# One stage of a graph network on Trainium2: harmonics of the plane products read from PSUM, fewer VectorE products, radial products scaled in place

## The reference, cut to what matters

```
out_s = [w_ss * s * y0,  w_vv0 * (dot(v, y1) / sqrt(3))]
out_v = [(w_sv * s) * y1,  w_vs * v * y0,  w_vv1 * (cross(v, y1) / sqrt(2))]
```

## Time and profile before

| what | us |
|---|---|
| median of three runs (6443.19 to 6455.58) | 6447.02 |
| the profiled execution | 6445.45 |
| its span | 6443.7 |
| DVE busy in the span (75%) | 4808.7 |
| PE busy (75%) | 4855.9 |
| POOL busy (66%) | 4230.3 |
| ACT busy (36%) | 2316.4 |

### The profile page before, as it was taken

One profiled execution on the slowest core, in us unless ns is written; L12 is line 12 of the kernel. 1 busy time (PEld: TensorE's weight loads), 2 busy tenths in 40 slices (PEclk: granted clock), 3 DMA queues, 4 the chain that ended last, 5 costly groups with the idle time before them and its releaser, 6 DMA issues. The chain is left out here.

```text
span 6443.7 us, 162517 instructions
## 1 busy us (share of the span) xinstructions
PE 4855.9 (75%) x45499; PEld 3778.9 (59%) x45500; DVE 4808.7 (75%) x11056; ACT 2316.4 (36%) x6999; POOL 4230.3 (66%) x4250
## 2 busy tenths in 40 slices
PE   6666667488888888888888769877766677777775
PEld 3444445377777777777777757644444464444445
DVE  5777776489989899898998764477777756666665
ACT  1100002266666666666666567400100021000001
POOL 5777775177767777777777347277777727777772
PEclk8888888699999999999999979888888887777777
DMA  3333332133333333333333247222222212222221
GB/s 108 92 92 92 92 92 69 44 94 90 92 89 92 92 89 92 90 91 92 89 92 90 66 148 229 61 73 72 72 72 72 72 38 69 69 69 69 69 69 38
DMA packets 401459, 545.15 MB, mean 85 GB/s; under 512 B 144998, under 2 KB 283382, under 8 KB 401244
## 3 DMA queue, kind: packets, MB, share of 16 engines
q0 software_dynamic: 193920, 331.22, 20.7%
q1 hardware_dynamic: 207452, 212.84, 11.3%
HBM read 464.79 MB, written 78.90 MB: 84 GB/s over the span
## 5 line engine op out<-in xcount | busy, mean ns | idle before, releaser
L816 POOL DMA_INDIRECT e_rows<-tab,e_idx x2424 | 2291.8, 945 | 814.1 <-issue 682.3
L1085 POOL DMA_INDIRECT acc<-tabx,a_idx x1616 | 1682.1, 1041 | 870.4 <-issue 465.2
L861 PE MATMUL e_wps<-e_w,e_hidT 64*128 64x192 f32 (+1 forms) x4848 | 792.9, 461 | 877.1 <-DVE e_hidT L932 874.5
L861 PEld LDWEIGHTS e_wps<-e_w,e_hidT 64*128 64x128 f32 x4848 | 539.7, 250 | 1081.1 <-DVE e_hidT L932 967.8
L846 PE MATMUL e_win<-e_feat,e_ohy 128*32 128x96 f32 (+1 forms) x19392 | 1026.5, 330 | 23.4 <-DVE e_feat L926 21.9
L846 PEld LDWEIGHTS e_win<-e_feat,e_ohy 128*32 128x32 f32 x19392 | 706.6, 131 | 454.2 <-issue 296.5
L917 DVE TENSOR_TENSOR e_feat<-e_wps,e_rows 128x256 f32<-128x256 f32 x606 | 257.3, 425 | 836.7 <-DMA e_rows<-tab,e_idx 758.7
L926 DVE TENSOR_TENSOR e_feat<-e_wps,e_rows 128x384 f32<-128x384 f32 (+1 forms) x1616 | 719.2, 496 | 0.0
L1148 PE MATMUL a_c<-acc,a_buffer 128*128 128x64 f32 (+1 forms) x4848 | 624.7, 272 | 121.8 <-ACT a_buffer L1126 121.8
L835 ACT ACTIVATE e_idx<-src 128x4 int32 (+1 forms) x606 | 123.3, 204 | 1603.1 <-DMA e_rows<-tab,e_idx 1580.1
L1148 PEld LDWEIGHTS a_c<-acc,a_buffer 128*128 128x128 f32 (+1 forms) x4848 | 590.3, 192 | 143.9 <-issue 143.9
(11 more groups left out here) (252 smaller groups left out, 7851.1 us busy)
## 6 DMA issues: line engine op xcount, KB each, us to landing
h_d<-a_buffer SPq DMA_DIRECT2D x202, 322.0 KB, 2.5
s_hin<-h_d SPq DMA_DIRECT2D x202, 322.0 KB
e_rows<-tab,e_idx POOLq DMA_INDIRECT x2424
e_ein<-in_e64T SPq DMA_DIRECT2D x202, 128.0 KB
acc<-tabx,a_idx POOLq DMA_INDIRECT x1616
a_ein<-in_e_h SPq DMA_DIRECT2D x202, 64.0 KB
e_ein<-in_e16T SPq DMA_DIRECT2D x202, 32.0 KB
tab<-p_rows SPq DMA_DIRECT2D x36, 160.0 KB
```

Source lines behind the costliest of these rows:

```text
L816: pool.indirect_dma_start(out=rows[:, s, t, :], out_offset=None, in_=k.tab0, in_offset=bass.IndirectOffsetOnAxis(ap=idx[:, s, t:t + 1], ax ...
L861: mm = pe.matmul(wps[:, e, 2 * u + j, 0:WC], hidT[half, edges], w2[half, :], start=True, stop=True)
L1085: pool.indirect_dma_start(out=rows[:, b, q, :], out_offset=None, in_=table, in_offset=bass.IndirectOffsetOnAxis(ap=idx[:, b, end, q:q + 1] ...
```

## The change: what it does

- The nine harmonics are laid out with one of them negated, so that one subtraction of planes gives two terms of the dot product or components of the cross product together: `y13_t` has 13 columns, of which 0 to 8 are the planes, 9 to 11 the plain harmonics, 12 is y0. ScalarE negates column 4 in SBUF once for each group, and waits for that write.
- `head` has eight operations: the add; one joint product for both scalar products (512 elements); the plane product with harmonics from `wps[224:233]`; the product for the w_vs part; one subtraction of 512 elements; the cross product's weights; an add of 128 elements; the dot product's weights.
- ScalarE scales the radial products in place in `wps` and copies the nine harmonics behind them. `wy` is gone.
- `mid` still has nine: the plane product reads its harmonics from `c2[192:201]`, and waits for `yc_ready`, which ScalarE signals after the copy that stands behind the scalars of the value row. The reduction and the two subtractions become two subtractions of 256 elements and an add of 128, which waits for the first of them.
- Two halves in `z` change places, and so do the rows of two weight matrices.

```diff
-    HEAD, MID, TAIL = 10, 9, 2
+    HEAD, MID, TAIL = 8, 9, 2
-        ybuf = scratch(U, TPG, 10)
+        ybuf = scratch(U, TPG, 13)
-        wy = scratch(TPG, 96)
-        vy, red, cr = scratch(TPG, 3, 3, V), scratch(TPG, V), scratch(TPG, 3, V)
+        vy, dc = scratch(TPG, 3, 3, V), scratch(TPG, 4, V)
...
                         act.activation(hrow[:, o, :, 0:S], c2[:, :, 0:S], ACT.Copy).then_inc(hs_ready, 1)
+                    if inside(g, n):
+                        if isinstance(g, int) and g == 1:
+                            hold(act, k, c2_ready, 1)
+                        act.activation(c2[:, :, 192:201], ybuf[:, s, :, 0:9], ACT.Copy).then_inc(yc_ready, 1)
                     take_feat((2,))
...
                         hold(act, k, y_in[b], uses(s, i, 2) * 16 + 16)
+                        act.activation(ybuf[:, b, :, 4], ybuf[:, b, :, 4], ACT.Copy, scale=-1.0).then_inc(minus_ready, 1)
+                        hold(act, k, minus_ready, g + 3)
                         hold(act, k, w_ready, g + 3)
                         for q in range(TPG):
-                            ins = act.activation(wy[:, q, :], wps[:, q, 0:96], ACT.Copy, scale=ybuf[:, b, q, 9:10])
+                            act.activation(wps[:, q, 0:96], wps[:, q, 0:96], ACT.Copy, scale=ybuf[:, b, q, 12:13])
+                        ins = act.activation(wps[:, :, 224:233], ybuf[:, b, :, 0:9], ACT.Copy)
                         ins.then_inc(wy_ready, 1)
...
                     hold(v, k, head_ops, at + 1)
-                    v.tensor_tensor(feat[:, :, 0:S], wy[:, :, 0:S], m[:, :, 0:S], ALU.mult).then_inc(head_ops, 1)
-                    with_planes(vy, mv, y).then_inc(head_ops, 1)
-                    v.tensor_tensor(feat[:, :, 96:160], wps[:, :, 96:160], m[:, :, 0:S], ALU.mult).then_inc(head_ops, 1)
+                    v.tensor_tensor(feat[:, :, 0:192].rearrange("p t (o c) -> p t o c", o=2)[:, :, :, 0:S],
+                                    wps[:, :, 0:192].rearrange("p t (o c) -> p t o c", o=2)[:, :, :, 0:S],
+                                    over(m[:, :, 0:S], 2, 2), ALU.mult).then_inc(head_ops, 1)
+                    with_planes(vy, mv, wps[:, :, 224:233]).then_inc(head_ops, 1)
+                    v.tensor_tensor(pair[:, :, :, 0:V], over(wps[:, :, S:96], 2, 3), mv, ALU.mult).then_inc(head_ops, 1)
                     hold(v, k, head_ops, at + 3)
-                    v.tensor_reduce(red[:, :, :], vy[:, :, 0, :, :].rearrange("p t x c -> p t c x"), AX.X, ALU.add).then_inc(head_ops, 1)
-                    v.tensor_tensor(pair[:, :, :, 0:V], over(wy[:, :, S:96], 2, 3), mv, ALU.mult).then_inc(head_ops, 1)
-                    cross(cr, vy, head_ops)
+                    of = turned_planes(vy)
+                    v.tensor_tensor(dc[:, :, :, :], of[:, :, 0:4, :], of[:, :, 4:8, :], ALU.subtract).then_inc(head_ops, 1)
                     hold(v, k, head_ops, at + 5)
-                    v.tensor_tensor(feat[:, :, S:96], wps[:, :, 160:192], red[:, :, :], ALU.mult).then_inc(head_ops, 1)
-                    hold(v, k, head_ops, at + 8)
-                    v.tensor_tensor(pair[:, :, :, V:2 * V], over(wps[:, :, 192:224], 2, 3), cr[:, :, :, :], ALU.mult).then_inc(head_ops, 1)
+                    v.tensor_tensor(pair[:, :, :, V:2 * V], over(wps[:, :, 192:224], 2, 3), dc[:, :, 1:4, :], ALU.mult).then_inc(head_ops, 1)
+                    v.tensor_tensor(dc[:, :, 0, :], dc[:, :, 0, :], of[:, :, 8, :], ALU.add).then_inc(head_ops, 1)
+                    hold(v, k, head_ops, at + 7)
+                    v.tensor_tensor(feat[:, :, S:96], wps[:, :, 160:192], dc[:, :, 0, :], ALU.mult).then_inc(head_ops, 1)
...
                     hold(v, k, mid_ops, at + 4)
-                    with_planes(ty, vec, y).then_inc(mid_ops, 1)
+                    hold(v, k, yc_ready, g + 1)
+                    with_planes(ty, vec, c2[:, :, 192:201]).then_inc(mid_ops, 1)
                     hold(v, k, mid_ops, at + 6)
                     if not isinstance(g, int) or g >= 2:
                         hold(v, k, z_turned, g * 3 - 3)
-                    v.tensor_reduce(zz[:, :, S:96], ty[:, :, 0, :, :].rearrange("p t x c -> p t c x"), AX.X, ALU.add).then_inc(mid_ops, 1)
-                    cross(pair[:, :, :, V:2 * V], ty, mid_ops)
+                    of = turned_planes(ty)
+                    v.tensor_tensor(zz[:, :, 2 * V:8 * V].rearrange("p t (u w) -> p t u w", u=2)[:, :, :, 0:V], of[:, :, 0:2, :],
+                                    of[:, :, 4:6, :], ALU.subtract).then_inc(mid_ops, 1)
+                    v.tensor_tensor(zz[:, :, 7 * V:11 * V].rearrange("p t (u w) -> p t u w", u=2)[:, :, :, 0:V], of[:, :, 2:4, :],
+                                    of[:, :, 6:8, :], ALU.subtract).then_inc(mid_ops, 1)
+                    hold(v, k, mid_ops, at + 7)
+                    v.tensor_tensor(zz[:, :, S:96], zz[:, :, S:96], of[:, :, 8, :], ALU.add).then_inc(mid_ops, 1)
...
-        "y10_t": edge(i["edge_attr_4"]).reshape(G, TPG, P, 4)[..., [1, 2, 3, 2, 3, 1, 3, 1, 2, 0]]...
+        "y13_t": edge(i["edge_attr_4"]).reshape(G, TPG, P, 4)[..., [1, 3, 1, 2, 2, 2, 3, 1, 3, 1, 2, 3, 0]]...
```

More of the change, by code:

```diff
@@ L1026, in attention_logits @@
         dst_in = [sem(f"a_dst_in{s}") for s in range(U)]
-        w_ready, wy_ready = sem("a_w_ready"), sem("a_wy_ready")
+        w_ready, wy_ready, yc_ready = sem("a_w_ready"), sem("a_wy_ready"), sem("a_yc_ready")
+        minus_ready = sem("a_minus_ready")
         head_ops, mid_ops, tail_ops = sem("a_head_ops"), sem("a_mid_ops"), sem("a_tail_ops")
@@ L1112, in step @@
                         for q in range(TPG):
[L1113 to L1114 removed]
+                            ins = act.activation(z[:, s % 2, q, 160:352].rearrange("p (x w) -> p x w", x=3)[:, :, V:2 * V], vec[:, q, :, :],
+                                                 ACT.Copy, scale=ybuf[:, s, q, 12:13])
                         ins.then_inc(vy_ready, 1)
@@ L1237, in with_planes, with turned_planes @@
                     return v.tensor_tensor(to[:, :, :, :, :].rearrange("p t j x c -> p t j (x c)"), over(of, 2, 3),
-                                           y[:, :, 0:9].unsqueeze(3).to_broadcast([P, TPG, 9, V]).rearrange("p t (j x) c -> p t j x c", j=3),
+                                           y.unsqueeze(3).to_broadcast([P, TPG, 9, V]).rearrange("p t (j x) c -> p t j x c", j=3),
                                            ALU.mult)
-                def cross(to, of, signal):
-                    v.tensor_tensor(to[:, :, 1:3, :], of[:, :, 1, ::-2, :], of[:, :, 2, 0:2, :], ALU.subtract).then_inc(signal, 1)
-                    v.tensor_tensor(to[:, :, 0:1, :], of[:, :, 1, 1:2, :], of[:, :, 2, 2:3, :], ALU.subtract).then_inc(signal, 1)
+                def turned_planes(of):
+                    return of.rearrange("p t j x c -> p t (j x) c")
                 def head(g, s, i):
@@ L1277, in mid @@
                     hold(v, k, sig_ready, g + 1)
-                    v.tensor_tensor(t[:, :, :, :], over(fv[:, :, 0:V], 2, 3), planes(y, 0), ALU.mult).then_inc(mid_ops, 1)
+                    v.tensor_tensor(t[:, :, :, :], over(fv[:, :, 0:V], 2, 3), planes(y, 9), ALU.mult).then_inc(mid_ops, 1)
                     v.tensor_tensor(lk[:, s % 2, :, :, 0:16], rect[:, s % 2, :, :].rearrange("p t (q c) -> p t q c", q=H),
@@ L1303, in tail @@
                     v.wait_ge(hs_ready, g + 1)
-                    v.tensor_tensor(t5[:, :, :, :], over(c2[:, :, S:96], 2, 3), planes(ybuf[:, s % U, :, :], 0), ALU.mult).then_inc(tail_ops, 1)
+                    v.tensor_tensor(t5[:, :, :, :], over(c2[:, :, S:96], 2, 3), planes(ybuf[:, s % U, :, :], 9), ALU.mult).then_inc(tail_ops, 1)
                     if not isinstance(g, int) or g >= 2:
@@ L1881, in _arrays @@
         "e64T": edge(i["edge_attr_64"]).T, "e16T": edge(i["edge_attr_16"]).T, "e8T": edge(i["edge_attr_8"]).T,
-        "y10_t": edge(i["edge_attr_4"]).reshape(G, TPG, P, 4)[..., [1, 2, 3, 2, 3, 1, 3, 1, 2, 0]].transpose(0, 2, 1, 3).reshape(G, P, TPG * 10),
+        "y13_t": edge(i["edge_attr_4"]).reshape(G, TPG, P, 4)[..., [1, 3, 1, 2, 2, 2, 3, 1, 3, 1, 2, 3, 0]].transpose(0, 2, 1, 3).reshape(G, P, TPG * 13),
         "ends_t": np.stack([edge(src).reshape(G, TPG, P), edge(dst, fill=N).reshape(G, TPG, P)], 1).transpose(0, 3, 1, 2).reshape(G, P, 2 * TPG),
@@ L1961, in _arrays @@
     a["L1_c3_c"] = const((96, 64), [(0, 0, (64, 64), 1), (64, 0, (32, 64), r3)])
+    riap = lambda r, c, m: [(r, c, m[2]), (r + V, c, m[1])]
     for name, m in (("L1_c4", three), ("L1_c4_f", factors), ("L1_c4_c", bent(three))):
-        a[name] = _place((P, 64), [(0, 0, m[0])] + pair(64, 32, m))
+        a[name] = _place((P, 64), [(0, 0, m[0])] + riap(64, 32, m))
     for name, m in (("L1_c5", three), ("L1_c5_f", factors), ("L1_c5_c", bent(three))):
-        a[name] = _place((P, 64), pair(0, 0, m) + pair(64, 32, m))
+        a[name] = _place((P, 64), riap(0, 0, m) + riap(64, 32, m))
     w = np.zeros((P, SLOTS, D), f)
```

7 lines of the change are left out of this document (3 added, 4 removed).

## The result

The changed kernel takes 6854.82 us (median of four runs, 6842.4 to 6864.17), the kernel before 6446.41: ratio 1.063, 95% interval 1.0609 to 1.065. That is 408 us more, inside the stated range and near its upper end; 258 were forecast. The profiled execution has a span of 6850.9.

What follows compares the result with a forecast made beforehand. VectorE's closed chain was taken as the bound, with ScalarE and TensorE's just as long. 3.63 + 9.46 = 13.09 us a round, 246 us more over 202 rounds, gave 6693; plus 12, 6705 us; range 6600 to 6890.

Steps and rivals of the forecast that it cites:

- (a): In `mid`, the second plane product waits for ScalarE's harmonics copy: 3.63 us from the head's end against 2.47, VectorE idle 1.16.
- the trip: From the head's end through TensorE and ScalarE, twice each, to VectorE's second plane product in `mid`: 3.63 us a round.
- (b): VectorE from the second plane product to the next head's end: 9.46 us, with 0.40 for two newly exposed own-write waits.
- VectorE as a closed chain: In the kernel before, VectorE waits almost only for its own writes, with gaps of 0.15 to 0.45 us; round 11.87 us.
- the chain over ScalarE and TensorE: Transposes and copies handing one PSUM tile back and forth, through the second map; just as long as VectorE's chain, 11.87 us.
- (c): ScalarE's additions ahead of the `z` copies: negation, its wait and harmonics copy into `wps`, some 0.47 us, hidden.
- the sign that was named for being wrong in (c): TensorE's waits for ScalarE, not for VectorE, coming ahead of the transposes of `feat`.
- The tie and the clock: Over the whole kernel, 12 us (0.06 a round) added because the chains tie and the clock may fall at times.
- Rival 2: TensorE's clock falls as its busy share drops to 0.77; low half the time, 6800 to 6940, taken as 6850; chance 0.12.
- the case that was held the likeliest: The new wait in `mid` lengthens VectorE's round to 13.09 us; 6705 us, own range 6670 to 6890, chance 0.75.
- The skill's rules: For VectorE, PSUM sources costing more would give about 6757; semaphores costing nothing, about 6624; the prediction followed neither.

Runs made afterwards that it cites:

- the repeated-matmul kernel: Changed kernel with the first map's three products of tile 0 done twice in each round; 6636.85 us, ratio 1.0302 to the kernel before.
- the chain edits alone: Kernel before with only TensorE's waits reordered and the scaling of the gated vectors split; ratio 1.0014 on a slower chip, repeats 1.0031 and 1.002.
- the 109: Gain over the kernel before with SBUF harmonics, negation moved, TensorE waits reordered, vector scaling split and head reordered, on the changed kernel: 6331.48 against 6440.51 us.
- the wait alone: Kernel before with only the harmonics copy into c2 and the second plane product reading it there, so waiting for it; 6980.48 us, ratio 1.0845.

## Why the prediction was right in kind and short in size

- **The new wait in `mid` (a), right.** It is there in nearly every round, behind ScalarE's copy, and taking it away from this place gives back 337 of 408 us. At full clock the trip is 3.72 us (head's end 2504.98 to 2508.70), 3.63 were summed; VectorE's idle time 1.23, 1.16 were summed.
- **VectorE from there to the next head's end (b), too long.** 9.11 us on average, 9.46 summed. The two exposed own waits are 0.15 us each (one is 2516.23 + 0.68 to 2517.05), not 0.20; and the gap between add and first product is 0.15 (2512.92 + 0.82 to 2513.89), not 0.45. At full clock the round is 12.85 us by the repeated-matmul kernel, 13.09 were summed.
- **VectorE as a closed chain, wrong.** The gap of 0.45 us ahead of the head's first product was read as a wait for VectorE's own add. That product also waits for ScalarE's radial scaling, and two further waits stand behind that one. In the kernel before it starts 0.53 us after the scaling has ended, at the median and within 0.01 us in most rounds, while the gap behind the add varies from 0.29 to 0.45 us in eight rounds of ten. Here the scaling ends at 2511.74 + 1.02 = 2512.76:

```profile
2513.29 0.42 DVE L1259 TENSOR_TENSOR acc<-acc 128x256 f32<-128x256 f32 x1 [0.44 <-DVE acc L1253]
```

  In the kernel without the harmonics copies the distance is again 0.53, and there the profile names ScalarE, because the scaling ends after the add:

```profile
2501.77 1.01 ACT L1123 ACTIVATE a_wps<-a_wps,acc 128x96 f32<-128x96 f32 x4 [0.21 <-ACT acc L1119]
...
2503.31 0.69 DVE L1260 TENSOR_TENSOR acc<-a_wps,acc 128x512 f32<-128x512 f32 x1 [0.62 <-ACT a_wps L1123]
```

  So the chain over ScalarE and TensorE set the round of the kernel before. VectorE, though the busiest engine, had slack: the gap is 0.39 us on average, and 0.15 where nothing but the own write is waited for, which leaves 0.24 us a round. By this estimate the chain edits alone could have gained at most some 50 us of the 109 before VectorE's own work bound.
- **ScalarE's additions (c), hidden as predicted, but the chain beside them isn't.** In the changed kernel ScalarE waits for TensorE ahead of the copies of `z`, so its additions cost nothing there. Where the wait in `mid` is gone they show: 71 us over before with both copies made and 48 with neither, in kernels that have the new head and `mid` too (0.47 us a round would be 95). But the sign that was named for being wrong in (c) did come: TensorE waits for ScalarE ahead of the second map, and the transposes of `feat` come behind that. They start 1.3 us behind the head's end there (median), and 0.26 in the repeated-matmul kernel, where 0.14 were summed. So at full clock the two chains nearly tie, and at the low one the second sets the round.
- **The tie and the clock, mis-sized.** This is the term that was too small: "To this I add 12 us (0.06 a round) because the chains tie and the clock may fall at times". The changed kernel with its TensorE kept busy stands 213 us lower, so the low clock costs about that: 1.05 us a round. The second chain has three more transposes in it than the trip, so it loses more by a low clock, and VectorE waits twice, for the harmonics (275 us) and for the sigmoids (126 us). Rival 2 described this and gave 6850, with a chance of 0.12. Its reason was a busy share that falls to 0.77, and that isn't tested: the measured 0.84 holds matmuls stretched by the low clock, and the work of before (0.85 of 11.87 us) in rounds of 13.85 would be 0.73 at full clock. What the trace shows ahead of the slow transposes is that TensorE stands idle for 0.79 us.
- **Luck.** The result lies in the range, but not by the case that was held the likeliest. Without the 12 us that case stood 246 us over before, where the repeated-matmul kernel stands 195; so its round at full clock was 51 us too long in all, and its price for the clock 201 too low. The two errors cancel in part. That rival 2's 6850 is off by 5 us is partly luck as well: it took the clock to be low in half of the rounds, and the granted 0.88 is less than that.
- **The skill's rules.** Plane products read with harmonics in PSUM last 1.344 and 1.354 us by their median, 1.350 before, as this view of the line in the changed kernel (minimum, median, maximum) shows: the Trainium skill's fixed cost for PSUM sources (VectorE: DVE Perf Modes, The TRN2 errata) isn't seen, as predicted. The Trainium skill (the same page, "The DRAIN you can't avoid") measured eight copies in a row to take the same time with a semaphore behind each as with one behind the last. No run here repeats that. What this trace shows is an operation that waits for the one directly ahead of it: it starts 0.15 us after that one's end, where one that waits for nothing starts 0.08 before. So of the 0.40 us that were summed for two such waits, 0.30 were real.

```profile
L1244 DVE TENSOR_TENSOR acc<-acc,a_wps x202: 1342/1344/1346, 1283.0 to 4067.2; 128x1152 f32<-128x1152 f32 x101
L1244 DVE TENSOR_TENSOR acc<-acc,a_c x202: 1353/1354/1356, 1305.7 to 4091.5; 128x1152 f32<-128x1152 f32 x101
```

## What to carry to other kernels

Before moving an operand, find where the engine that fills it stands in its own order at the time when the reader needs it; here a copy of 0.20 us stood behind two transposes and cost the reader 1.5 us in each round. When a change makes TensorE wait, price the clock too: here it cost as much again, and repeating matmuls was a cheap way to see that. Of several waits in a row, put last the one that comes last. And where a profile names one releaser for an operation with several waits, measure the distance to each candidate over many rounds: the one at a constant distance is the one that counts. The busiest engine needn't be the one that sets the round.

## What the runs showed of the hardware

- The granted clock of the stage fell from 1.00 to 0.88 (0.82 with the wait alone), and three redundant matmuls a round brought it back to 1.00 and took 213 us off the kernel. TensorE's busy share gave no warning: it was 0.84 to 0.86 at the lower clock and 0.85 at the full one, since four transposes last 1.06 us at the low clock and 0.60 at the full one.
- A wait behind one that is still open isn't free: with three in a row and the late one first, TensorE starts 0.54 us after what it waited for; with the late one last, 0.14. VectorE shows the same: its first product, with the late wait ahead of two others, starts 0.53 us after ScalarE's scaling has ended, and 0.15 us behind its own add where all else had come before.
- Over the whole stage, gathers last 1.04 us on average before, 0.98 in the changed kernel (median 0.95 in both), and single ones up to 2.1 us in kernels whose plane products read two operands from SBUF, 1.6 where one is in PSUM. In the kernel without the harmonics copies, a gather of over 1.3 us overlaps a plane product for 0.87 us on average, the others for 0.09. The Trainium skill (SBUF — State Buffer, section "Who interferes with whom") has VectorE's second SBUF input and GpSimd share a port; these rows agree, and freeing the port gained nothing here, as nobody waited for a gather.
